# Windowed attention scores per head on half of the rows, in four parts with halves of the q and V projections between them

## The chip, the cores and the metric

The kernel runs on one core of a Trainium2 chip. The metric is the device time of one execution in microseconds; lower is better. Its engines work side by side and meet only at semaphores: TensorE (PE in the profile, with its weight loads as PEld), VectorE (DVE), ScalarE (ACT), GpSimd (POOL) and SyncE (SP), which issues the DMAs.

## What is computed

A decoder block in float32 on x of shape (4, 512, 128): a self attention, a cross attention, and then six layers of windowed attention with a feed-forward part. Nearly all of the time is in the six layers:

```python
def local_attention(q, k, v):              # 16 heads of 64, windows of 32
    bk2, bv2 = (look(bk), look(bv))        # each window sees itself and the one before
    mask = (it < jb) | (it > jb + w) | (jb == -1)
    sim = jnp.einsum('bhwie,bhwje->bhwij', bq, bk2) * QK_SCALE
    sim = jnp.where(mask, -jnp.finfo(sim.dtype).max, sim)
    attn = jax.nn.softmax(sim, -1)
    out = jnp.einsum('bhwij,bhwje->bhwie', attn, bv2)

def attn_layer(x, Wqkv, qs, ksc, Wo):
    q, k, v = jnp.split(x @ Wqkv, 3, -1)   # 128 -> 3 x 1024
    q, k = l2norm(q) * qs, l2norm(k) * ksc # then rotary embedding with a scale
    return local_attention(q, k, v) @ Wo

for i in range(6):
    x = attn_layer(shift_tokens(x), ...) + x
    x = ffn_layer(shift_tokens(x), ...) + x    # layer norm, 128 -> 2 x 341, gated gelu, -> 128
```

## The kernel before

The layers are one software pipeline over `t`, a tile of 128 tokens (four windows) of one layer: 6 layers x 4 batches x 4 tiles = 96 tiles. Each engine has its own loop over the same steps, written out by hand, and runs its instructions in that order; a step does work of several tiles. On TensorE a step t is, in order: the k projection of tile t (L1239), the turn of the attention output of t-3 (L1301), the turns of q and k of t-1 (L1248), the q projection of t (L1239), the turn of the probabilities of t-2 (L1278), in some steps a mean over the features (L1330), the mask and scores of t-1 (L1263, L1268), the values of t-2 (L1290), the V projection of t (L1313). Every fourth step has the output projection of a batch (L1323) at its end; the next has the feed-forward's mean and variance (L1330); the next its hidden layer (L1342); the next its last matmul (L1352). These four kinds of step follow each other.

A float32 matmul of the program is two load/matmul pairs in the trace; a bf16 one and a transpose are one pair.

Scores: heads go in pairs. `qT` holds two heads' 64 features on 128 partitions. `kb`, the keys, holds the pair twice, once with each head's rows and zeros in the other's (`kb[:, t % 2, c, :, ...]`), so that one matmul for each pair c and window j gives both heads' scores, with 32 columns of weights (q), 128 moving columns (two times 64 keys) and all 128 rows. Its output goes to the window's 32 PSUM partitions. The four windows use four different 32-column strips of the array. The mask is added into PSUM ahead of them by two bf16 matmuls of 128 rows (`mask_sel`, `mask`; only 64 of the rows are used).

PSUM is four slots of two banks. A planner gives each product its slot by a fixed table, in the order of TensorE's program: slot 0 is for qT, pT, o and the third part of the hidden layer; slot 1 for k, mean, v (in this order within a step); slot 2 for oT, q, then wo, var, y; slot 3 for kT and s. `take(pe, key)` makes TensorE wait until the product before it in that slot has been read; `wait_full` and `wait_free` are the waits for a product's completion and for its reading. Only the last matmul of a product raises its semaphore.

What reads them: ScalarE squares k, copies out oT, qT and kT (L1449, L1393, L1427), squares q (L1401), copies pT, and so on. VectorE multiplies k by the cosines (L1528), sums the squares (L1519), does the sine part (L1540), then the same for q; in the step with a mean the subtraction of the mean (L1617, the centring, which frees the mean's slot) stands after q's sum of squares and before q's sine part. Then come the scores' maximum and subtraction (L1560, L1563) and the scaling of the output (L1580). GpSimd carries the last window's keys over into the next tile (L1201), then adds the sine parts (L1212) and applies the norms (L1215), for k and then for q; the turns of q and k in the next step wait for these.

## Time and profile before

| what | us |
|---|---|
| median of 3 runs | 2161.67 (2152.18 to 2171.68) |
| the profiled execution | 2155.05 |
| its span, first to last instruction | 2153.2 |
| TensorE busy, of the span | 2009.6 (93%) |
| VectorE busy | 1530.1 (71%) |
| ScalarE busy | 1311.6 (61%) |
| GpSimd busy | 988.3 (46%) |
| mean granted TensorE clock | 0.961 |

The profile is of one execution. A share of busy time says which engine is nearly always at work, not what a change in one place is worth; for that the timeline of the steps is read. The record of a matmul is longer than the time it keeps the next one waiting, as matmuls overlap: the distance from one start to the next is what counts. Busy TensorE time is therefore to be read as "not waiting".

### The profile page before, as it was taken

The numbers are of one execution on the slowest core, as the hardware profiler recorded it, in microseconds if no ns is written. First come the engines' busy times: TensorE is split into PE (matmuls) and PEld (weight loads), VectorE is DVE, ScalarE is ACT, GpSimd is POOL, SyncE is SP. The second block draws the span as 40 slices with busy tenths as digits, with TensorE's granted clock in tenths as the row PEclk, the third lists the DMA queues.
The fourth block names the chain that finished last, engine by engine and source line by source line (L and its number), as shares of the span: only waits on it lengthen the run. The fifth ranks groups of instructions, "written<-read, shape, count | busy, mean of one in ns | idle before, by whom it ended". The sixth has DMA issues, their size and how long they took to land. (4 is left out here: it accounts for less than half of the span.)

```text
span 2153.2 us, 46766 instructions
## 1 busy us (share of the span) xinstructions
PE 2009.6 (93%) x19016; PEld 1174.0 (55%) x19016; DVE 1530.1 (71%) x1741; ACT 1311.6 (61%) x1857; POOL 988.3 (46%) x715
## 2 busy tenths in 40 slices
PE   5799887769999999999999999999999999999996
PEld 2122122336666666666666666666666666666663
DVE  3889424548777877778777877778777777778762
ACT  3047784436666666667656766667666676666662
POOL 6000002246555655555555655555555555556540
PEclk9579998979999999999999999999999999999997
DMA  4510001025333345334443434433344433343340
GB/s 108 100 34 3 2 1 35 0 72 140 102 97 97 105 119 135 91 89 113 119 118 97 105 104 132 118 86 97 99 125 124 102 106 100 96 111 94 103 106 25
DMA packets 102357, 194.55 MB, mean 90 GB/s; under 512 B 12400, under 2 KB 32368, under 8 KB 102000
## 3 DMA queue, kind: packets, MB, share of 16 engines
q1 hardware_dynamic: 102144, 191.56, 34.0%
q8 instruction: 152, 2.49, 0.5%
q14 instruction: 61, 0.50, 0.1%
HBM read 123.77 MB, written 54.66 MB: 83 GB/s over the span
## 5 line engine op out<-in xcount | busy, mean ns | idle before, releaser
L1212 POOL TENSOR_TENSOR l_rot<-l_rot,l_rot_s 128x1024 f32<-128x1024 f32 x192 | 455.1, 2370 | 1.0 <-DVE l_rot_s L1540 1.0
L1201 POOL COPY l_kb<-l_kb 128x512 f32<-128x512 f32 x95 | 62.9, 662 | 693.1 <-ACT l_kb L1427 693.1
L1215 POOL TENSOR_TENSOR l_rot<-l_rot,l_norms 128x1024 f32<-128x1024 f32 x192 | 365.2, 1902 | 15.1
L1528 DVE TENSOR_TENSOR l_rot<-ps,l_tab_c 128x1024 f32<-128x1024 f32 x192 | 235.2, 1225 | 173.3 <-ACT l_sq L1401 173.3
L1401 ACT ACTIVATE l_sq<-ps 128x1024 f32<-128x1024 f32 x192 | 196.9, 1025 | 227.2 <-PE ps L1239 224.6
L1540 DVE TENSOR_TENSOR l_rot_s<-ps,l_tab_s 128x512 f32<-128x512 f32 x384 | 245.6, 681 | 0.0
L1519 DVE TENSOR_REDUCE l_norms<-l_sq 128x16 f32<-128x1024 f32 x192 | 232.2, 1209 | 0.0
L1239 PE MATMUL ps<-l_wqkv,xsT 128*128 128x512 f32 x384 | 188.3, 615 | 26.8 <-ACT l_v_tok L1393 15.5
L1427 ACT ACTIVATE l_kb<-ps 64x1024 f32<-64x1024 f32 x192 | 195.8, 1020 | 1.1
L468 ACT ACTIVATE probs<-ps 128x512 f32<-128x512 f32 x256 | 131.9, 605 | 102.8 <-PE ps L419 102.8
L1290 PE MATMUL ps<-l_vb,l_pT 128*32 128x128 f32 x6144 | 188.3, 274 | 1.6 <-ACT l_pT L1393 1.4
L1268 PE MATMUL ps<-l_kb,l_qT 128*32 128x128 f32 x6144 | 187.6, 274 | 0.0
L1239 PE MATMUL ps<-l_wqkv_odd,xsT 128*128 128x512 f32 x384 | 181.5, 595 | 4.9 <-ACT l_v_tok L1393 4.9
L1248 PE MATMUL ps<-cst,l_rot 128*128 128x128 f32 x1536 | 184.1, 273 | 0.0
L1268 PEld LDWEIGHTS ps<-l_kb,l_qT 128*32 128x32 f32 x6144 | 161.8, 110 | 40.7 <-issue 40.7
L1410 ACT ACTIVATE l_norms<-l_norms 128x16 f32<-128x16 f32 x192 | 41.6, 217 | 232.6 <-POOL l_norms L1209 232.6
L1290 PEld LDWEIGHTS ps<-l_vb,l_pT 128*32 128x32 f32 x6144 | 171.7, 111 | 2.6 <-ACT l_pT L1393 1.6
L1248 PEld LDWEIGHTS ps<-cst,l_rot 128*128 128x128 f32 x1536 | 171.5, 141 | 2.3 <-POOL l_rot L1215 1.2
L1323 PE MATMUL ps<-l_oT,l_wo 128*128 128x512 f32 x384 | 168.8, 593 | 1.2 <-ACT l_oT L1449 1.2
L478 DVE TENSOR_REDUCE mx<-ps 128x2 f32<-128x1024 f32 x128 | 149.7, 1218 | 12.7 <-PE ps L400 12.5
L831 POOL TENSOR_TENSOR x_kb<-x_kT,cst 128x512 f32<-128x512 f32 x4 | 4.1, 1045 | 304.9 <-DVE x_kT L895 304.9
L1393 ACT ACTIVATE l_v_tok<-ps 128x1024 f32<-128x1024 f32 x96 | 98.2, 1023 | 57.7 <-PE ps L1313 57.7
(165 smaller groups left out, 3352.1 us busy)
## 6 DMA issues: line engine op xcount, KB each, us to landing
l_vb<-v_scratch SPq DMA_DIRECT2D x336, 256.0 KB, 4.5
v_scratch<-l_v_tok SPq DMA_DIRECT2D x96, 512.0 KB, 4.8
l_vb<-v_scratch SPq DMA_DIRECT2D x48, 192.0 KB, 3.2
xsT<-xT SPq DMA_DIRECT2D x48, 135.8 KB, 2.5
stack<-scratch SPq DMA_DIRECT2D x96, 64.0 KB
l_xf<-xT SPq DMA_DIRECT2D x48, 128.0 KB, 2.4
l_wqkv_odd<-wqkv SPq DMA_DIRECT2D x9, 512.0 KB, 6.1
scratch<-parts SPq DMA_DIRECT2D x4, 768.0 KB, 11.3
```

The source lines that it names most:

```text
L1212: nc.gpsimd.tensor_tensor(rot[:, t % 2, n], rot[:, t % 2, n], rot_s[:, n], ALU.add).then_inc(added, 1)
L1215: nc.gpsimd.tensor_tensor(rot[:, t % 2, n], rot[:, t % 2, n], norms[:, t % 2, n, :, None].broadcast_to([P, HEADS, DH]), ALU.mult).then_inc ...
L1239: m = nc.tensor.matmul(slot(name, t)[:, c, :], xsT[:, b, PAD + i * P:PAD + (i + 1) * P], wqkv_sb[t // NT % 2][:, a:a + BANK], start=True, ...
L1248: m = nc.tensor.transpose(dst[:, c // 4, (c % 4) * P:(c % 4 + 1) * P], rot[:, t % 2, "qk".index(name), 2 * c:2 * c + 2, :], ident)
L1268: m = nc.tensor.matmul(dst[a:a + WINDOW, c // 4, (c % 4) * P:(c % 4 + 1) * P], qT[:, c, a:a + WINDOW], kb[:, t % 2, c, :, a:a + 2 * WINDOW ...
L1290: m = nc.tensor.matmul(dst[a:a + WINDOW, c // 4, (c % 4) * P:(c % 4 + 1) * P], pT[:, c, a:a + WINDOW], vb[:, j, :, c * DH:(c + 1) * DH], s ...
L1323: m = nc.tensor.matmul(slot("wo", b)[:, 0, :], wo_sb[:, c, :], oT[:, c, :], start=(c == 0), stop=(c == PAIRS - 1))
L1401: nc.scalar.activation(sq[:, 1 - r], slot(name, t).rearrange("p n (h d) -> p (n h) d", d=DH), ACT.Square).then_inc(squared, 1)
L1427: m = nc.scalar.activation(kb[rows, t % 2, :, parity, WINDOW:], src[rows, :, :], ACT.Copy)
L1519: nc.vector.tensor_reduce(half, sq[:, 1 - r], AX.X, ALU.add).then_inc(summed, 1)
L1528: nc.vector.tensor_tensor(rot[:, t % 2, 1 - r], slot(name, t).rearrange("p n (h d) -> p (n h) d", d=DH), tab_c[:, 1 - r, t % TILES, None, ...
L1540: m = nc.vector.tensor_tensor(rot_s[:, 1 - r, :, a:a + H2], raw[:, :, H2 - a:DH - a], tab_s[:, 1 - r, i, None, a:a + H2] .broadcast_to([P, ...
```

## The change

Scores are made for one head at a time. `kb` holds every key once (`[P, 2, PAIRS, WINDOW + P]`): the even head of a pair on partitions 0 to 63, the odd one on 64 to 127. A matmul takes the 64 rows of one head, 32 columns of q and 64 moving columns, and writes to bank n of the slot for parity n. Each pair and window so has two matmuls instead of one, 64 of the program in a step instead of 32. The scores' order in PSUM becomes (parity, pair), which `shift_scores` puts back while it subtracts. The mask is added by two bf16 matmuls of 64 rows, one for each bank, and its constants are laid out twice. The scores are issued in four parts of two pairs; between the parts stand the second half of the q projection and the two halves of the V projection of tile t, which stood ahead of the turn of the probabilities and behind the values. The key copy on ScalarE is one instruction of 128 rows instead of two of 64, GpSimd's carry moves half as much, and the zeroing of `kb` ahead of the layers is half as large. The slot table, and the order of the other engines' work, stay as they are.

```diff
         kept = dict(wqkv=sb("l_wqkv", [P, 3 * INNER]), scales=sb("l_scales", [P, 2, DH]),
-                    kb=sb("l_kb", [P, 2, PAIRS, 2, WINDOW + P]), vb=sb("l_vb", [P, WINDOWS, 2, PAIRS * DH]))
+                    kb=sb("l_kb", [P, 2, PAIRS, WINDOW + P]), vb=sb("l_vb", [P, WINDOWS, 2, PAIRS * DH]))
...
-                    nc.gpsimd.tensor_copy(kb[:, t % 2, :, :, 0:WINDOW],
-                                          kb[:, (t - 1) % 2, :, :, P:P + WINDOW]).then_inc(carried, 1)
+                    nc.gpsimd.tensor_copy(kb[:, t % 2, :, 0:WINDOW],
+                                          kb[:, (t - 1) % 2, :, P:P + WINDOW]).then_inc(carried, 1)
...
-                def project(name, t):
+                def project(name, t, c):
                     b, i = t // TILES % BATCH, t % TILES
                     part = "qk".index(name)
-                    if i == 0:
-                        wait(pe, xs_ready, 32 * (t // TILES + 1))
-                    if t % NT == 0:
-                        wait(pe, wqkv_ld[part], 16 * (t // NT))
-                    take(pe, name, t)
-                    for c in range(2):
-                        a = part * INNER + c * BANK
-                        m = nc.tensor.matmul(slot(name, t)[:, c, :], xsT[:, b, PAD + i * P:PAD + (i + 1) * P],
-                                             wqkv_sb[t // NT % 2][:, a:a + BANK], start=True, stop=True)
-                    m.then_inc(filled(name, t), 1)
+                    if c == 0:
+                        if i == 0:
+                            wait(pe, xs_ready, 32 * (t // TILES + 1))
+                        if t % NT == 0:
+                            wait(pe, wqkv_ld[part], 16 * (t // NT))
+                        take(pe, name, t)
+                    a = part * INNER + c * BANK
+                    m = nc.tensor.matmul(slot(name, t)[:, c, :], xsT[:, b, PAD + i * P:PAD + (i + 1) * P],
+                                         wqkv_sb[t // NT % 2][:, a:a + BANK], start=True, stop=True)
+                    if c == 1:
+                        m.then_inc(filled(name, t), 1)
...
-                def scores(t):
+                def open_scores(t):
 
                     wait_free(pe, "qT", t)
                     wait_free(pe, "kT", t)
                     wait(pe, carried, t)
                     if t == 0:
-                        pe.wait_ge(consts_set, 5)
+                        pe.wait_ge(consts_set, 3)
                     take(pe, "s", t)
                     dst = slot("s", t)
                     opening = int(t % TILES == 0)
                     for n in range(2):
-                        nc.tensor.matmul(dst[:, n, :], mask_sel[:, opening, :], mask[:, :], start=True, stop=False,
+                        rows = slice(64 * n, 64 * n + 64)
+                        nc.tensor.matmul(dst[:, n, :], mask_sel[rows, opening, :], mask[rows, :], start=True, stop=False,
                                          skip_group_check=True)
-                    for c in range(PAIRS):
+                def head_scores(t, part):
+
+                    dst = slot("s", t)
+                    for c in range(2 * part, 2 * part + 2):
                         for j in range(WINDOWS):
-                            a = j * WINDOW
-                            m = nc.tensor.matmul(dst[a:a + WINDOW, c // 4, (c % 4) * P:(c % 4 + 1) * P],
-                                                 qT[:, c, a:a + WINDOW], kb[:, t % 2, c, :, a:a + 2 * WINDOW],
-                                                 start=False, stop=True, skip_group_check=True)
-                    m.then_inc(filled("s", t), 1)
+                            a, at = j * WINDOW, 2 * c * WINDOW
+                            for n in range(2):
+                                rows = slice(64 * n, 64 * n + 64)
+                                m = nc.tensor.matmul(dst[a:a + WINDOW, n, at:at + 2 * WINDOW],
+                                                     qT[rows, c, a:a + WINDOW], kb[rows, t % 2, c, a:a + 2 * WINDOW],
+                                                     start=False, stop=True, skip_group_check=True)
+                    if part == 3:
+                        m.then_inc(filled("s", t), 1)
...
-                def project_v(t):
+                def project_v(t, parity):
 
                     b, i = t // TILES % BATCH, t % TILES
                     wv = wqkv_sb[t // NT % 2][:, 2 * INNER:].rearrange("p (c a d) -> p a c d", a=2, d=DH)
-                    if t % NT == 0:
-                        wait(pe, wqkv_ld[2], 16 * (t // NT))
-                    take(pe, "v", t)
-                    for parity in range(2):
-                        m = nc.tensor.matmul(slot("v", t)[:, parity, :], xsT[:, b, PAD + i * P:PAD + (i + 1) * P],
-                                             wv[:, parity], start=True, stop=True)
-                    m.then_inc(filled("v", t), 1)
+                    if parity == 0:
+                        if t % NT == 0:
+                            wait(pe, wqkv_ld[2], 16 * (t // NT))
+                        take(pe, "v", t)
+                    m = nc.tensor.matmul(slot("v", t)[:, parity, :], xsT[:, b, PAD + i * P:PAD + (i + 1) * P],
+                                         wv[:, parity], start=True, stop=True)
+                    if parity == 1:
+                        m.then_inc(filled("v", t), 1)
...
                     if has(t):
-                        project("k", t)
+                        project("k", t, 0)
+                        project("k", t, 1)
                     if has(t - 3):
                         turn_out(t - 3)
                     if has(t - 1):
                         turn("q", t - 1)
                         turn("k", t - 1)
                     if has(t):
-                        project("q", t)
+                        project("q", t, 0)
+                        if t == 0:
+                            project("q", t, 1)
                     if has(t - 2):
                         turn_probs(t - 2)
                     if b_norm is not None:
                         moment("mean", xf_ready, 32 * (b_norm + 1), b_norm)
                     if has(t - 1):
-                        scores(t - 1)
+                        open_scores(t - 1)
+                        head_scores(t - 1, 0)
+                        if has(t):
+                            project("q", t, 1)
+                        head_scores(t - 1, 1)
+                        if has(t):
+                            project_v(t, 0)
+                        head_scores(t - 1, 2)
+                        if has(t):
+                            project_v(t, 1)
+                        head_scores(t - 1, 3)
+                    if t == 0:
+                        project_v(t, 0)
+                        project_v(t, 1)
                     if has(t - 2):
                         values(t - 2)
-                    if has(t):
-                        project_v(t)
...
-                    src = slot("kT", t).rearrange("p n (c q) -> p (n c) q", q=P)
-                    for parity in range(2):
-                        rows = slice(64 * parity, 64 * parity + 64)
-                        m = nc.scalar.activation(kb[rows, t % 2, :, parity, WINDOW:], src[rows, :, :], ACT.Copy)
-                    m.then_inc(emptied("kT", t), 1)
+                    nc.scalar.activation(kb[:, t % 2, :, WINDOW:],
+                                         slot("kT", t).rearrange("p n (c q) -> p (n c) q", q=P), ACT.Copy)\
+                        .then_inc(emptied("kT", t), 1)
...
-                nc.vector.memset(mask[2 * WINDOW:, :], 0.0).then_inc(consts_set, 1)
-                nc.vector.memset(mask_sel[2 * WINDOW:, :, :], 0.0).then_inc(consts_set, 1)
-                nc.vector.tensor_copy(mask[0:2 * WINDOW, :], const("wmask")[0:2 * WINDOW, :]).then_inc(consts_set, 1)
-                nc.vector.tensor_copy(mask_sel[0:2 * WINDOW, :, :],
-                                      const("wsel")[0:2 * WINDOW, :].rearrange("p (a q) -> p a q", a=2))\
+                nc.vector.tensor_copy(mask[:, :], const("wmask")).then_inc(consts_set, 1)
+                nc.vector.tensor_copy(mask_sel[:, :, :], const("wsel").rearrange("p (a q) -> p a q", a=2))\
...
-                    nc.vector.tensor_reduce(mx[:, t % 2, :], s, AX.X, ALU.max).then_inc(maxed, 1)
+                    nc.vector.tensor_reduce(mx[:, t % 2], s, AX.X, ALU.max).then_inc(maxed, 1)
                     wait(dve, maxed, t + 1)
                     wait(dve, exped, t)
-                    nc.vector.tensor_tensor(dif[:, :, :], s,
-                                            mx[:, t % 2, :, None].broadcast_to([P, HEADS, 2 * WINDOW]),
+                    nc.vector.tensor_tensor(dif[:, :, :].rearrange("p (c n) k -> p n c k", n=2), s,
+                                            mx[:, t % 2, :, :, None].broadcast_to([P, 2, PAIRS, 2 * WINDOW]),
...
+    m[2 * WINDOW:] = m[:2 * WINDOW]
...
```

## Rows read from the trace of the kernel before

**Rows 1.** Busy time (and instructions) of each engine in one stretch, clock, DMA
```profile
core 0: us, PE busy (x) PEld busy (x) DVE busy (x) ACT busy (x) POOL busy (x), PEclk, DMA share, GB/s
489.00:2110.00 1621.00, 1600.69 (x17298) 1036.40 (x17298) 1237.49 (x1390) 1064.64 (x1426) 897.64 (x658) 1.00 0.41 107
```
**Rows 2.** Timeline of TensorE, from steps of three kinds (start, duration, what, count)
```profile
1005.30 1.04 PE L1278 MATMUL ps<-cst,l_prob 128*128 128x128 f32 x8
1006.37 0.59 PE L1263 MATMUL ps<-l_mask,l_mask_sel 128*128 128x512 bf16 x2
...
1008.66 1.93 PE L1290 MATMUL ps<-l_vb,l_pT 128*32 128x128 f32 x64
1010.52 1.98 PE L1313 MATMUL ps<-l_wqkv,xsT 128*128 128x512 f32 x4
...
1034.69 1.88 PE L1239 MATMUL ps<-l_wqkv,xsT 128*128 128x512 f32 x4
...
1040.75 1.04 PE L1278 MATMUL ps<-cst,l_prob 128*128 128x128 f32 x8
...
1049.88 1.96 PE L1239 MATMUL ps<-l_wqkv,xsT 128*128 128x512 f32 x4 [0.41 <-ACT l_v_tok L1393]
...
1068.02 1.88 PE L1239 MATMUL ps<-l_wqkv,xsT 128*128 128x512 f32 x4
...
1083.69 1.88 PE L1239 MATMUL ps<-l_wqkv,xsT 128*128 128x512 f32 x4
```
**Rows 3.** Timeline of TensorE in windows that end at 1006.92 and 1007.20
```profile
1006.89 0.32 PE L1268 MATMUL ps<-l_kb,l_qT 128*32 128x128 f32 x4
...
1006.89 0.54 PE L1268 MATMUL ps<-l_kb,l_qT 128*32 128x128 f32 x12
```
**Rows 4.** Timeline of TensorE, self attention, from column strips to 64-row matmuls
```profile
250.56 0.61 PE L431 MATMUL ps<-probs,vaug 128*32 128x512 f32 x4
251.10 0.39 PE L419 MATMUL ps<-stack 64*128 64x512 bf16 x2
```
**Rows 5.** TensorE sequencer's waits (ns; first, last start); then L1268 from 1250.79
```profile
L1096 PEldq EVENT_SEMAPHORE  x2: 51/51/51, 1228.2 to 1230.2; - x2
...
L1096 PEldq EVENT_SEMAPHORE  x2: 51/51/51, 1248.1 to 1250.7; - x2
...
1250.79:1253.00 2.21, 0.77 (x29) 0.50 (x20) 1.00 0.03 7
```
**Rows 6.** Timeline of ScalarE, VectorE and GpSimd in the mean/variance step from 1034.69
```profile
1036.61 1.03 ACT L1401 ACTIVATE l_sq<-ps 128x1024 f32<-128x1024 f32 x1 [6.56 <-PE ps L1239]
...
1039.33 2.05 ACT L1427 ACTIVATE l_kb<-ps 64x1024 f32<-64x1024 f32 x2
...
1041.41 1.02 ACT L1401 ACTIVATE l_sq<-ps 128x1024 f32<-128x1024 f32 x1
...
1039.94 1.28 DVE L1540 TENSOR_TENSOR l_rot_s<-ps,l_tab_s 128x512 f32<-128x512 f32 x2
1042.47 1.23 DVE L1528 TENSOR_TENSOR l_rot<-ps,l_tab_c 128x1024 f32<-128x1024 f32 x1 [1.25 <-ACT l_sq L1401]
...
1044.73 0.68 DVE L1617 TENSOR_TENSOR l_cen<-l_xf,ps 128x512 f32<-128x512 f32 x1
1045.33 1.28 DVE L1540 TENSOR_TENSOR l_rot_s<-ps,l_tab_s 128x512 f32<-128x512 f32 x2
...
1046.76 2.35 POOL L1212 TENSOR_TENSOR l_rot<-l_rot,l_rot_s 128x1024 f32<-128x1024 f32 x1
1049.19 1.90 POOL L1215 TENSOR_TENSOR l_rot<-l_rot,l_norms 128x1024 f32<-128x1024 f32 x1
```
**Rows 7.** Stretches with their clock (columns as rows 1), then timeline of TensorE there
```profile
474.70:478.20 3.50, 3.40 (x4) 1.35 (x5) 1.63 (x3) 1.11 (x2) 2.76 (x2) 0.51 0.37 150
...
2102.90:2106.30 3.40, 3.24 (x64) 3.22 (x64) 0.00 (x0) 0.01 (x1) 0.00 (x0) 0.50 0.02 5
...
474.80 3.64 PE L1239 MATMUL ps<-l_wqkv,xsT 128*128 128x512 f32 x4 [2.43 <-ACT l_v_tok L1393]
...
2103.06 3.52 PE L1290 MATMUL ps<-l_vb,l_pT 128*32 128x128 f32 x64 [1.40 <-ACT l_pT L1393]
```

More of the change, by code:

```diff
@@ L834, in _ @@
                 pool.memset(env["xsT"][:, :, 0:1], 0.0).then_inc(zeroed, 1)
-                pool.memset(kept["kb"][:, :, :, :, :], 0.0).then_inc(zeroed, 1)
+                pool.memset(kept["kb"][:, :, :, :], 0.0).then_inc(zeroed, 1)
                 pool.memset(kept["vb"][:, :, :, :], 0.0).then_inc(zeroed, 1)
@@ L986, in layers @@
         qT = sb("l_qT", [P, PAIRS, P])
-        mx = sb("l_mx", [P, 2, HEADS])
+        mx = sb("l_mx", [P, 2, 2, PAIRS])
         dif = sb("l_dif", [P, HEADS, 2 * WINDOW])
@@ L1408, in inverse_norm @@
                     if part == 0:
-                        act.wait_ge(consts_set, 5)
+                        act.wait_ge(consts_set, 3)
                     nc.scalar.activation(norms[:, t % 2, 1 - r], norms[:, t % 2, 1 - r], ACT.Ln, scale=65536.0)\
@@ L1557, in shift_scores @@
                 def shift_scores(t):
-                    s = slot("s", t).rearrange("p n (h k) -> p (n h) k", k=2 * WINDOW)
+                    s = slot("s", t).rearrange("p n (c k) -> p n c k", k=2 * WINDOW)
                     wait_full(dve, "s", t)
-                    nc.vector.tensor_reduce(mx[:, t % 2, :], s, AX.X, ALU.max).then_inc(maxed, 1)
+                    nc.vector.tensor_reduce(mx[:, t % 2], s, AX.X, ALU.max).then_inc(maxed, 1)
                     wait(dve, maxed, t + 1)
                     wait(dve, exped, t)
-                    nc.vector.tensor_tensor(dif[:, :, :], s,
-                                            mx[:, t % 2, :, None].broadcast_to([P, HEADS, 2 * WINDOW]),
+                    nc.vector.tensor_tensor(dif[:, :, :].rearrange("p (c n) k -> p n c k", n=2), s,
+                                            mx[:, t % 2, :, :, None].broadcast_to([P, 2, PAIRS, 2 * WINDOW]),
                                             ALU.subtract).then_inc(emptied("s", t), 1)
@@ L1689, in shape_constants @@
         s[q % WINDOW + (WINDOW if q < WINDOW else 0), 1, q] = 1.0
+    s[2 * WINDOW:] = s[:2 * WINDOW]
     put("wsel", s)
```

## The prediction

> **What bounds the kernel now.** I read the busy time of each engine first: between 489 and 2110 us, where the layers run, TensorE is busy 1600.7 of 1621.0 us at full clock while VectorE has 1237.5 and ScalarE 1064.6 [rows 1]. So a microsecond taken from TensorE in every step is worth about 96 us, one step being one token tile of one layer. The pace comes from the timeline of TensorE over one step of each kind [rows 2]. A step begins with the k projection; k, the turns and q take 6.06 us (1034.69 to 1040.75), then come the probability turn 0.87, mask 0.52, scores 1.77, values 1.86 and v, back to back. Four kinds follow each other: with the output projection, with mean and variance (1034.69, 15.19 us long), with the hidden layer (1049.88, 18.14), and with the last FFN matmul (1068.02, 15.67; the next starts at 1083.69). The only idle TensorE shows there is 0.41 us ahead of the k projection after the mean/variance step, and a 0.2 us late mask in the last kind (mask at 1006.37 where the turn from 1005.30 had ended by 1006.17).
>
> **Scores.** 64 matmuls in 1.77 us are 27.7 ns each. In narrow windows 4 of them have started by 1006.92 and 12 by 1007.20 [rows 3]: four start some 7 ns apart, one per window's column strip, and the next four 109 ns later. Sixteen waves of 0.109 are 1.75. Half the moving columns (64 for 128) make a wave of about 0.056, if nothing else limits, and eight tiles (two row halves by four strips) instead of four. The new form issues 128 matmuls and 128 loads a step instead of 64 and 64; 128 / 8 = 16 waves x 0.056 = 0.90 us, 0.22 for each of the four parts. Two row halves do overlap: bf16 matmuls of 64 rows into different banks stand two within one start (x2 at 251.10, in a window that ends at 251.15) [rows 4]. So the two mask matmuls cost 0.21 together instead of 0.43.
>
> **Changing the array's shape.** The mask starts 1006.37 and streams 0.43; scores start at 0.52, so the change from whole array to strips costs 0.09. Values last 1.86 for 1.75 of waves, so 0.11 to come back [rows 2]. Strips to row halves: 250.56 plus 0.43 of streaming, next matmul at 251.10, 0.11 [rows 4]. Values follow scores at once, in the same shape. Before, a step pays 0.09 and the exit of values. After, nine changes besides that exit: into the mask, into part 0, out and in again around each of three halves (six), and part 3 into values. At 0.10 that is 0.9 us. Bounds: nothing, and 0.13.
>
> **Feeding the array.** The sequencer's own waits show its speed. Between the two waits at 1228.2 and 1230.2, which are those ahead of the mask and ahead of values, it pushed 66 load/matmul pairs in 2.0 us [rows 5]: 30 ns a pair. Where the mask was late and it could run ahead, the waits are 2.6 us apart (1248.1, 1250.7) and just after the second 29 score matmuls and 20 loads are still in the records. About ten and four of these were running (records of 273 and 110 ns, a pair each 27 ns), so some 35 instructions, 17 or 18 pairs, is what stands queued when it is full. A part is 32 pairs. Behind a projection half (0.86 us, time for 29) only 18 can queue; the other 14 come at 29 ns: 0.41 us, so with the first starts a part takes 0.45 rather than 0.22. Bounds: 0.22 if the whole part queues, 0.95 if none does. I take 0.45 since it comes from the same instructions in the same place. The Trainium skill (TensorE: Matmul & The Clock Gate, the opening table) gives a queue of 64 instructions, exactly one part; by that a part would be 0.22, a case below. The rows hold about 35, so I go by them.
>
> **An ordinary step.** Before, mask and scores: 0.52 + 1.77 = 2.29. After: 0.9 of changes + 0.21 mask + 4 x 0.45 = 2.91. The projections keep their 1.72 each. **+0.62 us, x 96 = +60 us.** The key copy becomes one 128x1024 copy of 1.02 instead of two of 1.02 [rows 6], off the path except in the step with the late mask: -0.2 x 24 = -5 us. GpSimd's carry of the window and its fill of l_kb halve; both lie beside TensorE's work and nobody waits for them, and the added mask rows are cast while TensorE waits for its first tokens: nothing.
>
> **What moving q and v does.** q is complete only after mask, part 0 and a shape change. Chain of an ordinary step, from its start: mask ready at 6.07, part 0 from 6.48 to 6.93, q complete 7.9 (was 6.06), squares 8.1, cosines 9.15, then three more VectorE operations, 3.5 (from the cosines at 1042.47, less the centring's 0.6, to the sine part's end), to 12.65, and GpSimd's 2.4 + 1.9 to 17.0 [rows 6]. The turn of q is 2.6 into the next step, and the shortest of these steps is then 15.67 - 0.2 + 0.62 = 16.1 long, so it comes at 18.7 at the earliest. Hidden, with 1.7 to spare. v's slot is free of k by 6.6 and asked for at 8.5: hidden.
> Not so in the 23 steps with a mean (24 batches of a layer, the last mean after the last v). k, mean and v share slot 1, in this order, and taking it for v waits until the mean is read by the centring (L1617). VectorE has that behind cosines and squares' sum of q (L1528, L1519), which need all of q. Before, v came 1.2 us after the centring. Now, on the clock of the step at 1034.69 [rows 2, 6]: k's slot is free at 1041.22, mean 1041.3 to 42.15; mask and changes 0.41; part 0 0.45; change; q's half 1043.12 to 43.98; squares at 44.15 (k's came 0.2 after k's end); cosines one square later, 45.2; centring 2.26 after (as 42.47 to 44.73) at 47.45, done 48.13. v's first half can start at 48.2; TensorE is through part 1 at 44.6 and idles **3.55 us**. Then 0.86 + 0.65 + 0.86 + 0.65 + values 1.86 + variance 0.86 end at 53.9 instead of 49.88: +4.0, that is +3.4 beyond the +0.62. **x 23 = +78 us.** Queued behind the wait are parts 2 and 3, values, and so VectorE's maximum and the next step's outputs; these have their own slack, as the whole step slips.
>
> **The clock.** It was 1.00 through the layers, and fell to 0.50 for 3.4 us at 2102.9 with an idle of 1.40, and just ahead of the layers' steady part at 474.7 with an idle of 2.43 [rows 7]. These are the 1.2 and 2.4 GHz levels; at the lower 64 value matmuls took 3.52 instead of 1.93. An idle of 3.55 should do the same. 3.4 us at half speed lose up to 1.7, less where the low stretch begins inside the idle: 1.3 x 23 = **+30 us**. Bounds: 0 and 1.7.
>
> **Sum.** 60 - 5 + 78 + 30 = +163 us. The profiled execution was 2155.05 us (span 2153.2), 6.6 under the median of 2161.67; I add to the median: 2325 us, slower.
>
> **The rivals.**
> *Parts at wave speed* (the whole part queues behind its half). 0.9 + 0.21 + 0.9 - 2.29 = -0.28 a step, -27; the mean steps still idle 3.8, because the centring hangs on q's chain and not on TensorE: +85, clock +30, -5: about 2245. The rows' 35 speak against it, and a burst of four that starts 7 ns apart speaks for fast starts once queued. Chance 0.2. This is what the queue length of the Trainium skill named above would give.
> *The clock holds.* Two cases are few, and here TensorE is busy on both sides of the idle: 2325 - 30 = 2295. Chance 0.22.
> *Parts are not hidden at all* (0.95 each; a shape change also keeps the queue from filling): 2.0 more a step, 2162 + 252 + about 100 = 2515. Against it: pushing goes on while a matmul streams, as the waits show. Chance 0.06.
> *Faster: changes of shape cost nothing.* With parts at wave speed and no drain, mask and scores take 0.21 + 0.90: -1.18 a step, -113. With -5 and +80 for the mean steps it comes to 2124 without the clock, 2154 with it. Nine changes a step are 864: it turns into a gain below 0.04 us a change if the clock holds, below 0.01 if not. The three measured changes of 0.09 to 0.11 speak against it. Chance 0.06.
>
> **Numbers.** 0.46 for the forecast, whose own range is 2290 to 2370; 0.2, 0.22, 0.06 and 0.06 as above. 2230 to 2400 leaves out the faster and the unhidden case and some of the tails. About 1% is what a measurement here tells from none. Faster 0.05, same 0.04, slower 0.91.
>
> **What would show it.** Right: in 23 steps TensorE waits some 3.5 us, ahead of v's first half, for VectorE's centring; granted clock under 1 in the layers; in other steps some 2.9 us plus the three halves' 2.57 from the end of the probability turn to values. Wrong: no gap ahead of v in the mean steps; a part's 32 matmuls started within 0.25 us; a gap ahead of the q turn, which would mean that GpSimd's chain has become the bound; or a mask start still tied to the key copy.

## The result, and the profile after

The changed kernel takes 2313.64 us (median of 4 runs, 2308.63 to 2332.24) where the kernel before took 2156.93 beside it (2151.95 to 2171.68): ratio 1.0724, 95% interval 1.067 to 1.0778, slower by 7%. The profiled execution has a span of 2310.5 us against 2153.2. Runs of one kernel scatter by some 20 us, so below 1% I go by the lengths of the steps in the traces, which mostly repeat to 0.01 us (not in e2_unbroken and e8, nor in the mean steps of the changed kernel and of e3). One execution of e2_unbroken, 2395.42 us at a granted clock of 0.82 where the other three have 0.957 to 0.962, is left out of its figures. The code after has other line numbers: project L1239, turns of q and k L1249, mask L1265, scores L1275, probability turn L1286, values L1298, v L1321, mean and variance L1339, hidden layer L1351, squares L1424, cosines L1546, centring L1635.

The page's first part:

```profile
PE 2076.1 (90%) x25160; PEld 1098.7 (48%) x25160; DVE 1528.5 (66%) x1739; ACT 1219.7 (53%) x1761; POOL 972.2 (42%) x715
```

Busy times in one stretch of the layers (columns as in [rows 1]):

```profile
490.00:2000.00 1510.00, 1424.11 (x19873) 821.20 (x19866) 1061.38 (x1194) 831.28 (x1139) 765.55 (x571) 0.98 0.37 100
```

TensorE was busy 98.7% of [rows 1]; here it is 94.3%, at a mean clock of 0.98. So 86 us of this stretch are idle, and some of the rest is at half speed. The waits of the whole run name who is waited for (engine, what <- whom: total us, times, longest):

```profile
PEld ps L1321 <- DVE l_cen L1635: 89.0, 23, 3.9
PE ps L1321 <- DVE l_cen L1635: 85.3, 23, 3.7
DVE l_mx L1578 <- PE ps L1275: 84.9, 24, 4.7
```

23 waits of 3.7 us, ahead of v, for the centring: one in each mean step. The second line of VectorE is its echo: the maximum waits for scores that stand queued behind that v. Here is such a step on TensorE's timeline, from its k projection to the next one:

```profile
1311.01 1.88 PE L1239 MATMUL ps<-l_wqkv,xsT 128*128 128x512 f32 x4
...
1317.68 1.10 PE L1339 MATMUL ps<-l_xf,cst 128*128 128x512 f32 x2 [0.44 <-DVE l_rot_s L1558]
1318.71 0.39 PE L1265 MATMUL ps<-l_mask,l_mask_sel 64*128 64x512 bf16 x2
1319.03 0.46 PE L1275 MATMUL ps<-l_kb,l_qT 64*32 64x64 f32 x32
1319.42 1.13 PE L1239 MATMUL ps<-l_wqkv,xsT 128*128 128x512 f32 x2
1320.47 0.46 PE L1275 MATMUL ps<-l_kb,l_qT 64*32 64x64 f32 x32
1324.64 1.54 PE L1321 MATMUL ps<-l_wqkv,xsT 128*128 128x512 f32 x2 [3.71 <-DVE l_cen L1635]
1326.11 0.68 PE L1275 MATMUL ps<-l_kb,l_qT 64*32 64x64 f32 x32
1326.71 2.06 PE L1321 MATMUL ps<-l_wqkv,xsT 128*128 128x512 f32 x2
1328.70 0.45 PE L1275 MATMUL ps<-l_kb,l_qT 64*32 64x64 f32 x32
...
1331.93 1.02 PE L1239 MATMUL ps<-l_wqkv_odd,xsT 128*128 128x512 f32 x2
```

VectorE in the same step:

```profile
1321.63 1.23 DVE L1546 TENSOR_TENSOR l_rot<-ps,l_tab_c 128x1024 f32<-128x1024 f32 x1 [4.10 <-ACT l_sq L1424]
1322.78 1.21 DVE L1537 TENSOR_REDUCE l_norms<-l_sq 128x16 f32<-128x1024 f32 x1
1323.90 0.68 DVE L1635 TENSOR_TENSOR l_cen<-l_xf,ps 128x512 f32<-128x512 f32 x1
```

The stretch right behind the wait (columns as in [rows 1]; the clock is the third from the end):

```profile
1325.20:1328.60 3.40, 3.40 (x36) 0.93 (x34) 0.58 (x1) 0.57 (x3) 2.61 (x3) 0.50 0.00 0
```

The q projection ends at 1320.4, its squares let the cosines start at 1321.63, the centring stands behind cosines and sum and ends at 1324.58, and v starts at 1324.64. Then TensorE works through 3.40 us at 0.50 of its clock (1.2 GHz), with 100% busy time: v's halves take 1.47 and 1.99 us instead of 1.06. The clock fell in all 22 mean steps between 550 and 2170 us. The low stretch begins between 0.5 us before v starts and 1.35 after; in 19 steps it lasts 3.4 us, in three 6.8, and those three steps took 22.2 us instead of about 20.9.

The four kinds of step, medians in us from one k projection to the next (some 20 of each kind), for all kernels of this study:

| kernel | hidden layer | last FFN | output projection | mean/variance | cycle |
|---|---|---|---|---|---|
| before | 18.13 | 15.67 | 19.77 | 15.20 | 68.77 |
| after | 18.68 | 15.78 | 20.05 | 20.86 | 75.37 |
| e4_mask64 | 18.02 | 15.47 | 19.66 | 15.09 | 68.24 |
| e6_mask64_split_copy | 18.02 | 15.47 | 19.66 | 14.60 | 67.75 |
| e1_centre_first | 19.51 | 15.78 | 20.05 | 15.85 | 71.19 |
| e5_fill_idle | 18.68 | 15.78 | 20.05 | 19.35 | 73.86 |
| e2_unbroken | 18.60 | 16.08 | 19.97 | 15.55 | 70.20 |
| e3_parts_of_old_scores | 20.03 | 17.53 | 21.54 | 22.61 | 81.71 |
| e8_v_before_values | 18.08 | 15.24 | 19.53 | 14.38 | 67.23 |
| e7_v_in_the_middle | 18.08 | 15.40 | 19.69 | 14.54 | 67.71 |
| e9_v_middle_old_order | 17.97 | 15.40 | 19.69 | 15.86 | 68.92 |

After against before: 24 x (0.55 + 0.11 + 0.28) = 22.6, 23 x 5.66 = 130, together 153 of the 157 us between the spans; the three long mean steps, 1.4 each, make up the other 4. So 85% of the loss sits in one step of four.

The changed middle of an ordinary step on TensorE's timeline:

```profile
1337.13 1.04 PE L1286 MATMUL ps<-cst,l_prob 128*128 128x128 f32 x8
1338.10 0.39 PE L1265 MATMUL ps<-l_mask,l_mask_sel 64*128 64x512 bf16 x2
1338.42 0.45 PE L1275 MATMUL ps<-l_kb,l_qT 64*32 64x64 f32 x32
1338.81 1.12 PE L1239 MATMUL ps<-l_wqkv_odd,xsT 128*128 128x512 f32 x2
1339.86 0.45 PE L1275 MATMUL ps<-l_kb,l_qT 64*32 64x64 f32 x32
1340.24 1.12 PE L1321 MATMUL ps<-l_wqkv_odd,xsT 128*128 128x512 f32 x2
```

The first part again, in windows that end at 1338.50, 1338.55 and 1338.70:

```profile
1338.42 0.29 PE L1275 MATMUL ps<-l_kb,l_qT 64*32 64x64 f32 x8
...
1338.42 0.34 PE L1275 MATMUL ps<-l_kb,l_qT 64*32 64x64 f32 x16
...
1338.42 0.45 PE L1275 MATMUL ps<-l_kb,l_qT 64*32 64x64 f32 x32
```

Eight have started by 1338.50, 16 by 1338.55, all 32 by 1338.66 (from the single records): 0.24 us, four waves some 55 ns apart. From part to projection is 0.38, from the start of a projection half to the next part 1.05 instead of 0.86.

### The profile page after: what moved, and what is told of

It is laid out like the page before. It is cut to its first block and busy times, and to the rows that moved or that the text cites. A ratio compares the mean times of both kernels' runs of the same rounds, so it can differ in the third digit from the quotient of the medians.

```text
span 2310.5 us, 58956 instructions
## 1 busy us (share of the span) xinstructions
PE 2076.1 (90%) x25160; PEld 1098.7 (48%) x25160; DVE 1528.5 (66%) x1739; ACT 1219.7 (53%) x1761; POOL 972.2 (42%) x715
## 5 line engine op out<-in xcount | busy, mean ns | idle before, releaser
L1546 DVE TENSOR_TENSOR l_rot<-ps,l_tab_c 128x1024 f32<-128x1024 f32 x192 | 234.8, 1223 | 323.1 <-ACT l_sq L1424 323.0
L1424 ACT ACTIVATE l_sq<-ps 128x1024 f32<-128x1024 f32 x192 | 196.5, 1024 | 436.8 <-PE ps L1239 436.0
L1201 POOL COPY l_kb<-l_kb 128x256 f32<-128x256 f32 x95 | 37.7, 397 | 648.5 <-ACT l_kb L1447 648.5
L1275 PEld LDWEIGHTS ps<-l_kb,l_qT 64*32 64x32 f32 x12288 | 117.7, 110 | 260.8 <-issue 260.8
L1239 PE MATMUL ps<-l_wqkv,xsT 128*128 128x512 f32 x384 | 198.3, 620 | 21.2 <-ACT l_v_tok L1416 10.7
L1298 PE MATMUL ps<-l_vb,l_pT 128*32 128x128 f32 x6144 | 192.6, 278 | 2.8 <-issue 1.4
L1239 PE MATMUL ps<-l_wqkv_odd,xsT 128*128 128x512 f32 x384 | 193.4, 605 | 0.0
L1249 PE MATMUL ps<-cst,l_rot 128*128 128x128 f32 x1536 | 186.6, 275 | 1.3 <-POOL l_rot L1215 1.3
L1275 PE MATMUL ps<-l_kb,l_qT 64*32 64x64 f32 x12288 | 182.0, 230 | 0.1
L1249 PEld LDWEIGHTS ps<-cst,l_rot 128*128 128x128 f32 x1536 | 173.3, 142 | 4.3 <-POOL l_rot L1215 3.2
L1578 DVE TENSOR_REDUCE l_mx<-ps 128x16 f32<-128x1024 f32 x96 | 116.9, 1217 | 84.9 <-PE ps L1275 84.9
L1298 PEld LDWEIGHTS ps<-l_vb,l_pT 128*32 128x32 f32 x6144 | 166.0, 112 | 13.3 <-issue 3.6
L1321 PE MATMUL ps<-l_wqkv_odd,xsT 128*128 128x512 f32 x192 | 123.9, 731 | 44.5 <-DVE l_cen L1635 44.5
L1455 ACT ACTIVATE l_prob<-l_dif 128x1024 f32<-128x1024 f32 x96 | 101.5, 1057 | 113.8 <-DVE l_dif L1581 113.8
L1321 PE MATMUL ps<-l_wqkv,xsT 128*128 128x512 f32 x192 | 120.2, 712 | 43.8 <-DVE l_cen L1635 40.8
```

The lines of the kernel that those rows point to most:

```text
L1239: m = nc.tensor.matmul(slot(name, t)[:, c, :], xsT[:, b, PAD + i * P:PAD + (i + 1) * P], wqkv_sb[t // NT % 2][:, a:a + BANK], start=True, ...
L1249: m = nc.tensor.transpose(dst[:, c // 4, (c % 4) * P:(c % 4 + 1) * P], rot[:, t % 2, "qk".index(name), 2 * c:2 * c + 2, :], ident)
L1275: m = nc.tensor.matmul(dst[a:a + WINDOW, n, at:at + 2 * WINDOW], qT[rows, c, a:a + WINDOW], kb[rows, t % 2, c, a:a + 2 * WINDOW], start=Fa ...
L1298: m = nc.tensor.matmul(dst[a:a + WINDOW, c // 4, (c % 4) * P:(c % 4 + 1) * P], pT[:, c, a:a + WINDOW], vb[:, j, :, c * DH:(c + 1) * DH], s ...
L1321: m = nc.tensor.matmul(slot("v", t)[:, parity, :], xsT[:, b, PAD + i * P:PAD + (i + 1) * P], wv[:, parity], start=True, stop=True)
L1424: nc.scalar.activation(sq[:, 1 - r], slot(name, t).rearrange("p n (h d) -> p (n h) d", d=DH), ACT.Square).then_inc(squared, 1)
```

## The experiments

Nine kernels besides the changed one. Those of one group ran on one chip, beside the kernel before.

**Is the centring's place what the mean steps pay for?** e1_centre_first is the changed kernel with VectorE's order in mean steps turned round:

```diff
-                    if has(t):
-                        cosine_part(t, 1)
-                        sum_squares(t, 1)
                     if b_norm is not None:
                         wait_full(dve, "mean", b_norm)
...
                             .then_inc(emptied("mean", b_norm), 1)
+                    if has(t):
+                        cosine_part(t, 1)
+                        sum_squares(t, 1)
```

> The changed kernel, with one order altered on VectorE: in the steps with a mean, the centring that frees PSUM slot 1 comes ahead of q's cosines and sum of squares instead of behind them. Slot theory: v's first half then finds its slot free, the idle of 3.7 us ahead of it and the 3.4 us at half clock behind it both go, the mean steps fall from 20.86 to about 15.5 us, the other steps stay, and the time falls by some 120 us to about 2190. Rival, that the long step is the late q itself (GpSimd's rotation of q and the next turn): the idle moves to the turn of q and the time stays above 2290.

Measured: 2213.93 us, 1.0259 (1.0209 to 1.0309), 100 us less than the changed kernel. Mean steps fell from 20.86 to 15.85, the granted clock in the layers is 1.00 again and no wait of TensorE for the centring is left. Most of it is as expected, but 2190 was not reached: the step after, the hidden layer's, grew from 18.68 to 19.51. The kernel's waits between 490 and 2000 us name two that the changed kernel did not have:

```profile
PEld ps L1309 <- DVE l_o_tok L1598: 30.5, 24, 1.4
PE ps L1309 <- ACT l_rstd L1516: 11.3, 20, 0.6
```

Both are ahead of the turn of the outputs, 1.7 us into the step, and the second ends last. In the step from 1292.35 VectorE's outputs are written by 1294.18, but the turn starts at 1294.87:

```profile
1293.09 1.06 ACT L1455 ACTIVATE l_prob<-l_dif 128x1024 f32<-128x1024 f32 x1 [0.89 <-DVE l_dif L1581]
1294.05 0.67 ACT L1516 ACTIVATE l_rstd<-ps,eps 128x512 f32<-128x512 f32 x1
1294.87 1.06 PE L1309 MATMUL ps<-cst,l_o_tok 128*128 128x128 f32 x8 [0.56 <-ACT l_rstd L1516]
```

The turn's slot still holds the variance. ScalarE reads it behind its exponential, and that waited for VectorE's difference from the maximum. The 0.8 us x 24 = 20 are most of the miss; the rest is that mean steps fell to 15.85 and not to 15.5. The slip of the mean steps had been the slack of that work.

**Does the clock cost what was said?** e5_fill_idle is the changed kernel with work that nobody reads in the idle time:

```diff
                         head_scores(t - 1, 1)
+                        if b_norm is not None and has(t):
+                            for _ in range(4):
+                                nc.tensor.matmul(slot("mean", b_norm)[:, 1, :], ident,
+                                                 xsT[:, t // TILES % BATCH, PAD:], start=True, stop=True)
```

> The changed kernel with four further 128x512 matmuls in each of the 24 mean steps, between part 1 and v's first half, where PE stood idle for 3.7 us waiting for the centring. Nothing reads what they write (the unused half of the mean's slot), so no data and no wait of another engine changes. It separates two terms of the forecast: the wait itself (3.4 us, which stays here) and the half clock that follows it. If the idle time is what makes the granted clock fall, the clock stays at 1.00 in every step, the matmuls behind the wait run at full speed, mean steps come down by about 1.3 us (20.86 to 19.5) and the kernel by 23 x 1.3 = 30 us: 2283, ratio to before about 1.058. The rival, that the clock falls once a cycle of four steps whatever stands in the gap, keeps the clock at 0.946 and the kernel at 2313 (1.072).

Measured: 2284.75, ratio 1.055 (1.0496 to 1.0605) against the changed kernel's 1.0724. The added matmuls and the v that follows:

```profile
1319.28 3.70 PE L1391 MATMUL ps<-xsT,cst 128*128 128x512 f32 x8
1323.06 1.12 PE L1321 MATMUL ps<-l_wqkv,xsT 128*128 128x512 f32 x2
```

The stretch around that v (columns as in [rows 1]):

```profile
1323.00:1326.00 3.00, 2.94 (x72) 1.25 (x76) 1.20 (x2) 1.43 (x4) 2.29 (x3) 1.00 0.02 5
```

v starts 13.62 us into the step as it did in the changed kernel, so behind it nothing but the clock differs. It stays at 1.00, and the mean step is 1.51 us shorter: 35 us a run, or 39 with the three long steps, which are not there either. A TensorE that does more work finishes sooner. The rival, a fall that comes once a cycle whatever stands in the gap, is out.

**The mask by itself.** e4_mask64 is the kernel before with the mask's two matmuls on 64 rows each (the mask's edits of the diff alone).

> The kernel before with the mask alone changed: two bf16 matmuls of 64 rows, in different row halves and banks, its constants laid out twice. Streaming falls from 0.43 to 0.21 us and one array change of 0.10 ahead of it is added: -0.1 us a step, -10 us, ratio 0.995. Rival, that the second change costs as much as is saved: ratio 1.000.

Measured: 2155.32, 0.9961 (0.9923 to 0.9998); mask to scores 0.32 instead of 0.52, steps 0.11 shorter, with the last FFN matmul 0.20 (the other 0.10 is a change of the array's shape that now also stands ahead of the mask: the probability turn before it takes 0.97 instead of 0.87). As expected.

**The per-head matmuls without the moves.** e2_unbroken is the changed kernel with the four parts in one stretch, q whole at its old place and v after the values.

```diff
-                        head_scores(t - 1, 0)
-                        if has(t):
-                            project("q", t, 1)
-                        head_scores(t - 1, 1)
...
+                        for part in range(4):
+                            head_scores(t - 1, part)
                     if has(t - 2):
                         values(t - 2)
+                    if has(t):
+                        project_v(t, 0)
+                        project_v(t, 1)
```

> The changed kernel with its per-head matmuls of 64 rows, but in one stretch: both halves of q stand at their old place ahead of the probability turn, both halves of v at theirs behind the values. No halves between, so no idle in the mean steps and no fall of the clock. If the sequencer feeds only a pair each 29 ns once what is queued has gone, the scores take 32 pairs at wave speed and 96 x 0.029 = 2.8 us, about 3.0 in all against 1.77, and the time is about 2160 + 96 x 1.1 = 2265. Rival, that feeding is no limit and waves of eight go at 0.056 throughout: 0.9 us, and about 2075.

Measured: 2178.76 (median of three, 2176.16 to 2196.28), 1.0111 (1.0048 to 1.0175). Both theories fell. A step from its timeline:

```profile
1262.73 1.49 PE L1275 MATMUL ps<-l_kb,l_qT 64*32 64x64 f32 x128
1264.14 1.95 PE L1298 MATMUL ps<-l_vb,l_pT 128*32 128x128 f32 x63
1266.82 0.27 PE L1298 MATMUL ps<-l_vb,l_pT 128*32 128x128 f32 x1 [0.73 <-issue]
```

128 loads and 128 matmuls pass in 1.41 us, 11 ns a pair: the array is fed nearly three times as fast as the 30 ns that I had read. In all 87 steps looked at, the first 32 of the 128 start within 0.24 us and the other 96 take about 1.03. Without a gap a step is 0.44 us shorter than before or more (19.33 against 19.77 with the output projection), but in two steps of three comes a gap in which no engine is named as waited for. Between 490 and 2000 us:

```profile
PE ps L1298 <- issue: 32.9, 43, 1.5
...
PE ps L1275 <- issue: 12.9, 15, 1.2
```

58 gaps of 0.8 us in some 86 steps; those steps come out about 1 us longer than the others. The kernel before has 1 such entry, of 0.2 us. The records of the DMA queue that the page calls "instruction" go with them. Between 1264.3 and 1265.4 us, ahead of the gap shown, it moved one packet (count, MB, share):

```profile
q8 instruction: 1, 0.02, 6.1%
```

This packet of 16 KB started at 1264.35 and took 1.07; TensorE resumed at 1266.82. Each of the 58 gaps ends 2.2 to 2.8 us after the start of such a packet, though the packets come only every 9 us or so. From one gap to the next TensorE does 250 to 253 matmuls with their loads, or a multiple of half of that. So the gaps belong to the delivery of TensorE's program; that is read off the trace, as no kernel changed the delivery. The new form issues 192 pairs a step in one stretch, with no long matmul behind which such a pause could hide.

**The moves without the per-head matmuls.** e3_parts_of_old_scores is the kernel before with its 64 128-row matmuls in four parts, and the halves of q and v between them as in the changed kernel (mask whole, key copies two).

> The kernel before with its own score matmuls (128 rows, a pair of heads each) and its own key layout, but issued in four parts with the halves of q and v between them as in the changed kernel. It isolates what the move costs. If each inserted half costs about 0.3 us of array changes whatever the scores' form, ordinary steps grow by 0.9 us; if the wait in the mean steps is a matter of order alone it is here too, 3.5 us and the clock: together about +190, 2350. Rival, that idle and changes belong to the 64-row form: within 20 us of before.

Measured: 2442.31, 1.1324 (1.1267 to 1.1381), 6.0 points beyond the changed kernel and 92 us over what I expected. A part takes 0.57 where the per-head one takes 0.38, and a wait is there that I had not priced, together with the known one (490 to 2000 us):

```profile
PE ps L1264 <- ACT l_kb L1447: 53.9, 57, 1.1
PE ps L1318 <- DVE l_cen L1637: 63.3, 18, 3.5
```

q's first half ends 0.86 earlier than the whole, so the mask comes earlier, and the key copies, two of 1.02 us [rows 6], are late by 0.95 in 57 of some 75 steps. These are all but the mean steps, where the mean's matmuls stand ahead of the mask. So the changed kernel needs its single key copy in three kinds of step, and not only in the one where the copy was late before. The idle ahead of v is the same with the old matmuls: it belongs to the move.

**One break instead of three.** e7_v_in_the_middle is the changed kernel with the centring first, q whole, and this order:

```diff
+                        head_scores(t - 1, 0)
+                        head_scores(t - 1, 1)
+                    if has(t):
+                        project_v(t, 0)
+                        project_v(t, 1)
+                    if has(t - 1):
+                        head_scores(t - 1, 2)
+                        head_scores(t - 1, 3)
```

> The changed kernel with its per-head matmuls, but q whole at its old place, v's two halves together between parts 1 and 2, and the centring ahead of q's cosines in mean steps. One break in the scores instead of three. By the terms measured on the changed kernel: unbroken scores without an issue gap are 0.44 us shorter than before, one break costs about 0.3, so an ordinary step is 0.15 shorter than before; the stretch of per-head matmuls never reaches 128, so TensorE's instructions are fed while projections run and the issue gap of 1 us once a step is covered in part. Mean steps no longer wait for the centring and the clock stays at 1.00. Sum: 96 x -0.15 less 9 at the mask and 5 elsewhere: 2130 to 2150, ratio 0.99 to 0.998. The rival, that the issue gap is not hidden by a break, gives each step its 1 us back: about 2190, ratio 1.015, as with the scores in one stretch.

e8_v_before_values has the same centring and q, all four parts in one stretch, then v, then the values:

> The changed kernel with its per-head matmuls in one stretch, q whole at its old place, v between the scores and the values, and the centring ahead of q's cosines in mean steps. It differs from the one with unbroken scores by v's place and by the centring. If the 1 us issue gap is sequencer time that long matmuls can cover, v's two matmuls (0.86 us) ahead of the 64 of the values cover part of it: 2150 to 2170, ratio 0.998 to 1.006. If the gap falls inside the scores as often as before, nothing is covered: about 2187 (1.011) with v earlier, less what the mean steps gain.

e6_mask64_split_copy is e4 with ScalarE's copy of v cut in two in mean steps:

```diff
+                        if parity == 0 and pieces(t)[1] is not None:
+                            m.then_inc(v_half, 1)
...
+                        act.wait_ge(v_half, pieces(t)[1] + 1)
+                        nc.scalar.activation(v_tok[:, 0, :], slot("v", t)[:, 0, :], ACT.Copy)
+                        copy_slot(("v", t), v_tok[:, 1, :], slot("v", t)[:, 1, :])
```

> The kernel before with the mask on 64 rows, and with ScalarE's copy of v in two halves in mean steps, the first released by v's first matmul. If v's copy is what the mean step's later work waits for, as its 0.4 us ahead of the mean suggests, mean steps fall by 0.4 us beside the 0.11 of every step: 96 x 0.11 + 23 x 0.41 = 20 us, 2136, ratio 0.991. The rival: the copy is not on that path, and the kernel gives the 0.996 of the mask alone, 2148.

Measured, on one chip with the kernel before at 2168.96 (11 runs, 2150.83 to 2176.88): e7 2121.61, ratio 0.9838 (0.9785 to 0.9891); e6 2133.23, 0.9877 (0.983 to 0.9924); e8 2143.04, 0.9895 (0.984 to 0.995). All three beat both kernels, by the steps too (table). e6 is where it was expected; e7 and e8 are 8 and 7 us below their ranges, in which I had no term for the wait that follows. The lowest times are 2119.92, 2129.14, 2127.05 and, before, 2150.83. A mean step of e7 on TensorE, from the mask to the next step:

```profile
1229.56 0.39 PE L1265 MATMUL ps<-l_mask,l_mask_sel 64*128 64x512 bf16 x2
1229.88 0.86 PE L1275 MATMUL ps<-l_kb,l_qT 64*32 64x64 f32 x64
1230.66 1.98 PE L1321 MATMUL ps<-l_wqkv,xsT 128*128 128x512 f32 x4
1232.58 0.86 PE L1275 MATMUL ps<-l_kb,l_qT 64*32 64x64 f32 x64
1233.37 1.96 PE L1298 MATMUL ps<-l_vb,l_pT 128*32 128x128 f32 x64
1235.25 1.13 PE L1339 MATMUL ps<-l_xf,cst 128*128 128x512 f32 x2
1236.21 1.02 PE L1239 MATMUL ps<-l_wqkv_odd,xsT 128*128 128x512 f32 x2
```

No idle anywhere here: 64 pairs in 0.79, v in 1.92 for 1.82, and k at once behind the variance. In the kernel before this is where TensorE waited 0.41 for ScalarE's copy of v [rows 2]. In e7 v is complete 3.6 us before k asks for the slot, and in e6 half of v has been copied when its second half ends; both take the wait away. The mask and that wait, and not the scores, are what e7 gains in its cycle: with the old scores the mask's 64 rows take 0.53 off the cycle (e4) and the wait another 0.49 (e6), which makes 67.75, and e7 has 67.71. What its profiled execution is shorter than e6's, 7 us, lies mostly in a few irregular steps: three that have none of the four extra pieces of work (about 13.0 us against 14.2) and three last-FFN steps of 16.2 to 16.4 in e6.

In e8 the gap comes back in part, 17 times between 490 and 2000 us, 15 of them in the scores. In e7 it comes not once, though the packets of the queue "instruction" come there too (177 in this stretch). The medians of e8's steps add up to the shortest cycle of all, but they leave the gaps out: with means it is 68.0 against e7's 67.7.

```profile
PE ps L1275 <- issue: 13.1, 15, 1.6
```

**The early v by itself.** e9_v_middle_old_order is e7 with VectorE's order as in the kernels before and after.

> The version with v's two halves between parts 1 and 2 and q whole, but VectorE's centring left behind the cosines and squares' sum of q, as in the kernels before and after. It prices the early place of v by itself, with q no longer late. In the kernel before, the centring of a mean step ended 10.7 us after the step's start; q is as early here, so it should end there again, while v asks for its slot at 9.0: an idle of 1.75 us in 23 mean steps, 40 us on 2122, so 2162, and if an idle of this length lowers the clock, up to 30 more, 2192 (ratio 1.00 to 1.015). The rival is that q's late completion alone made the 3.7 us of the changed kernel: then nothing is waited for here and the kernel stays at 2122, 0.984.

Measured: 2149.74 (10 runs), 0.9952 (0.9924 to 0.998), so 28 us more than e7, which ran on another chip. The wait is there, in 21 steps between 490 and 2000 us, and shorter than I worked out (1.3, not 1.75):

```profile
PE ps L1321 <- DVE l_cen L1629: 26.3, 21, 1.3
```

One of them on the timeline, in a step that began at 1250.57:

```profile
1260.88 1.98 PE L1321 MATMUL ps<-l_wqkv,xsT 128*128 128x512 f32 x4 [1.25 <-DVE l_cen L1629]
```

Mean steps of 15.86 against 14.54 give 1.32 x 23 = 30. The clock stayed at 1.00 in the layers, with an idle of 1.3 in each of them. With q on time the centring ends 10.3 us into the step, with q late 13.6; v's slot is asked for at 9.0 here and at 9.8 in the changed kernel. So of the changed kernel's 3.7 us all but 0.5 come from q's completion being late; and the longer idle alone brought the clock down. Both rivals of this run, nothing waited for and a lowered clock, fell.

## Why the prediction was right

The forecast was 2325 for 2313.6. The direction and the mechanism stood; the sizes of its terms were off in opposite directions, and part of the agreement is luck: ordinary steps were put 34 us too high, and mean steps, clock and hidden-layer steps together 24 to 28 too low.

**The mean steps: right.** The chain from q's half through squares, cosines, sum and centring was to end 13.44 us into the step, with an idle of 3.55 ahead of v. It ended at 13.57, with an idle of 3.71, in 23 steps. Even the mean's start, held by the sine part of k until 6.6, came at 6.67. e1 (take the order away, lose 5 us a mean step) and e3 (same idle with other matmuls) show that it is the cause. What I put on it, 3.4 beyond an ordinary step, was 5.66 - 0.27 - 1.51 = 3.9.

**The clock: right, a little small.** 1.3 x 23 = 30 forecast, 1.51 x 23 = 35 by e5, 39 with the three long steps. "The clock holds" at 0.22 was a fair rival, since the rows of before had two cases only.

**An ordinary step: the term that failed.** +0.62 forecast, +0.11 to +0.55 measured, +0.27 where nothing else interferes (the output projection's). The step of the argument at fault is "Feeding the array". I took 66 pairs between two waits of the sequencer, 2.0 us [rows 5], for the rate at which it can issue. It was the rate at which the array let it: 64 score matmuls took 1.77 us, 28 ns each [rows 2], and with a full queue the sequencer can go no faster than they do. e2 shows 11 ns a pair where the array asks for less. And a whole part does queue behind a projection half. It starts within 0.24 us, which the prediction itself had named as a sign of being wrong, and in e2 exactly 32 of the 128 start at that pace in every step before it drops. The Trainium skill (TensorE: Matmul & The Clock Gate, the opening table) has a queue of 64 instructions, exactly a part; the trace agrees with it, and my 35, counted from what was left in the records, does not stand. So "parts at wave speed" was right about the queue; it gave -0.28 a step, where +0.27 came, because at 0.10 a change it put the changes of shape too low.

By its terms: a part 0.29 with its last wave, not 0.45 (four: 1.16 for 1.80). The changes of shape cost more than 0.10 each. Out of a half and back: 0.09, then 0.10, and 0.10 more in the half itself, whose second matmul starts 533 ns after the first instead of 427 (also in the first pair of every hidden-layer stage behind the values: 533 instead of 429, where e2 with v between them has 430). So three halves cost 0.29 x 3 = 0.87 for changes rather than 0.60. Mask, parts, changes: 2.57 for the forecast's 2.91 and 2.29 before. The number of breaks then shows in the last-FFN steps: three 15.78, one 15.40, none 15.24 with v ahead of the values: 0.16 to 0.19 a break.

**The late mask: right.** The last-FFN kind is 0.16 better than the output projection's (+0.11 against +0.27), forecast 0.2.

**Not foreseen: the hidden-layer step,** +0.55. The hidden layer's second pair of matmuls goes to the scores' slot, which is free when VectorE has taken the difference from the maximum. VectorE comes to it behind cosines, sum and sine part of q, which are all late with q:

```profile
1345.01 5.77 PE L1351 MATMUL ps<-l_xg,l_w 128*128 128x512 f32 x12
...
1343.29 1.28 DVE L1558 TENSOR_TENSOR l_rot_s<-ps,l_tab_s 128x512 f32<-128x512 f32 x2
1344.49 1.22 DVE L1578 TENSOR_REDUCE l_mx<-ps 128x16 f32<-128x1024 f32 x1
1345.73 1.23 DVE L1581 TENSOR_TENSOR l_dif<-ps,l_mx 128x1024 f32<-128x1024 f32 x1
...
1347.08 0.73 PEld L1351 LDWEIGHTS ps<-l_xg,l_w 128*128 128x128 f32 x3 [0.91 <-issue]
```

Here are TensorE's matmuls, VectorE's difference, and the load of the fifth matmul. The fifth of the twelve starts 0.71 after the fourth instead of 0.43, its load at 1347.08, 0.12 after the difference ends. In e7, with q on time, the difference ends 13.9 us into such a step instead of 15.0, and the fifth starts after 0.43. The profile names nobody for this wait ("issue"); the slot plan and the times do, but it was not tried by itself. I had followed q, v and the mean through their slots, and not the scores' own slot behind VectorE's late work on q. It costs 24 x 0.28 = 7 us.

**q's turn: right.** The chain that I gave 1.7 us to spare never held TensorE in the layers: no wait for GpSimd's last factor is among those of the changed kernel between 490 and 2000 us.

**The sum again:** 26 for ordinary steps instead of 60, -4 at the mask, +7 in the hidden-layer steps, 90 and 35 for the mean steps instead of 78 and 30: 154, and 4 for the three long mean steps: 158, of 157 in the profiled executions.

## What to carry to other kernels

When a producer is moved later or a consumer earlier, write down for each buffer slot who has it before, and where the releasing operation stands in its engine's order: here a centring of 0.68 us, two places too far back, cost more than all the new matmuls. A rate read from the trace is a capacity only if nothing downstream sets it. And when an order of matmuls costs more at each change of shape than its cover is worth, make one break and not three, and move what is waited for ahead first.

## What the hardware showed that I had not expected

- Matmuls of 64 rows by 32 columns with 64 moving columns start 7 ns apart (32 in 0.24 us), and 128 of them with their loads in 1.41 us. The Trainium skill (TensorE: Matmul & The Clock Gate, "Wait — 56ns, not 53.3ns?") says that start-to-start never drops below about 25 ns; over different tiles of the array this trace shows less, while the waves, which come back to the same tiles, stay 55 ns apart.
- With two short stretches run together, TensorE's issue pauses for 0.8 us (58 times in some 86 steps of e2), each time 2.2 to 2.8 us after the start of a 16 KB packet on the queue "instruction", and at places of the program that lie some 250 load and matmul pairs apart. Long matmuls cover it: v in the midst of the scores left no gap (e7), v behind them 17 (e8).
- Idles of TensorE of 1.3 us in each mean step left the clock at 1.00 (e9), and idles of 3.7 us brought it to 0.50 in all 22 mean steps looked at, for 3.4 or 6.8 us. The stretch began between 0.5 us before the work resumed and 1.35 after, so that nearly all of it was paid for. The length of the last idle alone does not tell: ahead of the fall at 2102.9 us in the kernel before [rows 7], the idle of 1.40 us followed one of 0.78 that had ended 1.1 us earlier.
